# Routing logits and ranks moved to another PSUM bank and to other steps of the attention turns

## The reference, cut to what matters

```
x = LN(x + attention0(x))      16 heads of 64, causal, 2 null keys per head, l2-normed q and k, ALiBi
x = LN(x + moe0(x))            router of 8 experts, argmax: each row goes to one expert
x = LN(x + attention1(x))      squared-distance attention over the 4 batches
x = LN(x + moe1(x))            16 experts, top 2, and a shared one
```

## Time and profile before

| | us |
|---|---|
| median of 3 runs | 1722.08 |
| lowest, highest | 1718.21, 1733.55 |
| the profiled execution, its own time | 1720.87 |
| its span, first to last instruction | 1719.2 |
| TensorE busy | 1524.1 (89%) |
| VectorE busy | 1022.5 (59%) |
| ScalarE busy | 767.5 (45%) |
| GpSimd busy | 533.0 (31%) |
| mean granted TensorE clock | 0.929 |

### The profile page before, as it was taken

One profiled execution on the slowest core, in us unless ns is written; L12 is line 12 of the kernel. 1 busy time (PEld: TensorE's weight loads), 2 busy tenths in 40 slices (PEclk: granted clock), 3 DMA queues, 4 the chain that ended last, 5 costly groups with the idle time before them and its releaser, 6 DMA issues. The chain is left out here.

```text
span 1719.2 us, 26245 instructions
## 1 busy us (share of the span) xinstructions
PE 1524.1 (89%) x8079; PEld 704.2 (41%) x8079; DVE 1022.5 (59%) x2227; ACT 767.5 (45%) x1425; POOL 533.0 (31%) x589
## 2 busy tenths in 40 slices
PE   4899999999999999999999999998399439999997
PEld 2343344444444344443443434344277324444432
DVE  6455555655566664666555576565433267788774
ACT  3445454454544554544354454544044224444432
POOL 2043341533534444244353424432200321111000
PEclk8899899999999999998899999989599759999999
DMA  3503030320202202022020200000411100000000
GB/s 113 180 1 94 7 100 1 113 71 1 71 6 73 90 1 71 1 71 73 5 77 1 72 13 1 10 2 6 164 52 55 34 12 7 13 13 13 7 6 13
DMA packets 106708, 73.73 MB, mean 43 GB/s; under 512 B 5249, under 2 KB 100761, under 8 KB 106318
## 3 DMA queue, kind: packets, MB, share of 16 engines
q1 hardware_dynamic: 104526, 67.85, 13.1%
q0 software_dynamic: 2048, 4.20, 0.8%
HBM read 24.32 MB, written 47.71 MB: 42 GB/s over the span
## 5 line engine op out<-in xcount | busy, mean ns | idle before, releaser
L868 ACT ACTIVATE P<-S,keyb 128x258 f32<-128x258 f32 (+10 forms) x572 | 305.6, 592 | 401.5 <-PE S L635 294.3
L635 PE MATMUL S<-QT,KT 64*128 64x512 f32 (+5 forms) x1792 | 370.1, 494 | 7.1 <-DVE KT L1053 5.6
L1328 POOL TENSOR_SCALAR_AFFINE_SELECT P<-P 128x256 f32<-128x256 f32 (+1 forms) x256 | 162.0, 633 | 494.3 <-ACT P L868 493.6
L1095 DVE TENSOR_TENSOR Psum<-Psum,P 128x1796 f32<-128x1796 f32 (+7 forms) x256 | 283.1, 1106 | 43.6 <-POOL P L1328 30.5
L662 PE MATMUL O<-P,V 128*64 128x512 f32 (+5 forms) x1536 | 263.7, 448 | 4.5 <-POOL P L1328 3.9
L635 PEld LDWEIGHTS S<-QT,KT 64*128 64x128 f32 (+1 forms) x1792 | 161.0, 185 | 231.2 <-issue 227.3
L1305 POOL TENSOR_TENSOR rn<-nm,half 128x8 f32<-128x8 f32 (+1 forms) x120 | 220.6, 1842 | 90.7 <-DVE R L1008 47.3
L496 PE MATMUL W<-xT,wts 128*128 128x512 f32 x256 | 142.1, 650 | 10.1 <-DVE QT L1049 6.8
L662 PEld LDWEIGHTS O<-P,V 128*64 128x64 f32 (+1 forms) x1536 | 82.0, 139 | 113.9 <-issue 100.2
L1162 DVE TENSOR_TENSOR part<-W,rden 128x512 f32<-128x512 f32 x128 | 82.5, 686 | 77.1 <-PE W L711 76.1
L868 ACT ACTIVATE Psum<-S,keyb 128x1024 f32<-128x1024 f32 (+5 forms) x84 | 70.9, 911 | 125.9 <-issue 64.2
(11 more groups left out here) (263 smaller groups left out, 2006.7 us busy)
## 6 DMA issues: line engine op xcount, KB each, us to landing
xg<-zero SPq DMA_DIRECT2D x16, 1216.0 KB, 10.3
yg<-zero SPq DMA_DIRECT2D x16, 1216.0 KB, 9.3
wts<-in_w_qkv SPq DMA_DIRECT2D x16, 384.0 KB, 4.1
gu<-in_gu SPq DMA_DIRECT2D x1, 2816.0 KB
xb<-xg SPq DMA_DIRECT2D x40, 64.0 KB, 1.8
yg<-yb SPq DMA_DIRECT2D x40, 64.0 KB, 1.6
X<-in_x SPq DMA_DIRECT2D x4, 512.0 KB, 5.5
wo<-in_w_out SPq DMA_DIRECT2D x16, 128.0 KB, 2.4
```

The source lines that it names most:

```text
L635: last = nc.tensor.matmul(S[hh][0:m, at + c:at + c + w], KT[d, r, p, jt * P:jt * P + m], QT[d, r, p, Q0[jt] + c:Q0[jt] + c + w], start=Tru ...
L868: last = nc.scalar.activation(probs(p, jt)[0:m, hh, lo:hi], S[hh][0:m, at + lo:at + hi], ACT.Exp, bias=keyb[0:m, r, col:col + 1])
L1095: nc.vector.tensor_tensor(x, x, probs(p, jt)[0:m, :, 0:NQ[jt]], ALU.add).then_inc(add_ok, 1)
L1328: nc.gpsimd.affine_select(own, own, [[0, 2], [1, w]], ALU.is_ge, 0.0, base=NNULL if jt == 0 else 0, channel_multiplier=-1).then_inc(cut, 1)
```

## The change

Three lines are changed. XL moves from step 14a, bank 0, to step 10b, bank 1. XK moves from step 15b, bank 0, to step 14b, bank 1. These are the steps and the bank of E0 and E1. The row sums turned in step 11 (`masses_turned`, bank 1) now wait, in a routing turn, until XL is emptied, that is until the pick is done.

```
             AT = {"P00": "0b", "P01": "0b", "P02": "1b", "P03": "2a", "N0": "3b", "T0": "4b", "V3": "4b", "P10": "5a", "P11": "5b",
-                  "P12": "6a", "P13": "6b", "V0": "7a", "XR": "7b", "V1": "8a", "N1": "8b", "T1": "9b", "V2": "9b", "E0": "10b",
-                  "R0": "11a", "S00": "12b", "S01": "12b", "S02": "13b", "S03": "13b", "XL": "14a", "E1": "14b",
-                  "R1": "15a", "XK": "15b", "S10": "16a", "S11": "16b", "S12": "18a", "S13": "18a"}
-            BANK = dict(zip(AT, (0, 1, 1, 0, 0, 0, 1, 1, 0, 1, 0, 1, 0, 0, 1, 0, 1, 1, 0, 0, 1, 0, 1, 0, 1, 0, 0, 1, 0, 0, 1)))
+                  "P12": "6a", "P13": "6b", "V0": "7a", "XR": "7b", "V1": "8a", "N1": "8b", "T1": "9b", "V2": "9b", "E0": "10b", "XL": "10b",
+                  "R0": "11a", "S00": "12b", "S01": "12b", "S02": "13b", "S03": "13b", "E1": "14b", "XK": "14b",
+                  "R1": "15a", "S10": "16a", "S11": "16b", "S12": "18a", "S13": "18a"}
+            BANK = dict(zip(AT, (0, 1, 1, 0, 0, 0, 1, 1, 0, 1, 0, 1, 0, 0, 1, 0, 1, 1, 1, 0, 0, 1, 0, 1, 1, 1, 0, 1, 0, 0, 1)))
...
                     if ahead:
-                        k = PREP_BEFORE[p][1]
-                        pe.wait_ge(prep_ev[1], emptied(t + 1 + p, k if k in jobs(t + 1 + p) else "V2"))
+                        n = t + 1 + p
+                        k = next(j for j in ("XL", "E0", "V2") if j in jobs(n)) if p == 0 else PREP_BEFORE[p][1]
+                        pe.wait_ge(prep_ev[1], emptied(n, k))
```

## The result

| | us |
|---|---|
| changed kernel, median of 20 runs | 1732.41 (1724.32 to 1740.4) |
| kernel before, median of 20 runs | 1724.5 (1717.11 to 1733.55) |
| ratio | 1.0045, 95% interval 1.003 to 1.0059 |
| profiled execution of the changed kernel | 1727.98, span 1726.2, clock 0.926 |

The change makes the kernel slower by 0.45%, some 8 us. The forecast was 1721 with a range to 1730.

A forecast was written before the change was run, and what follows sets the result against it. Bounds: TensorE around step 10, then VectorE's pace before R1 and the ranks, and the granted clock. Gains of 2 x 0.12 + 4 x 0.15 = +0.8 us took the median from 1722.08 to 1721 us, range 1712 to 1730.

The forecast's parts named there:

- R1's and the ranks' waits: TensorE's idle 1.93 us before R1 and 0.55 before the ranks would go; S10 would wait 2.2 to 2.5 us instead.
- S02 to S10: Stretch from step 13's scores to the first spreading matmul of step 16: forecast 7.4 to 7.8 us, against 8.70 in turn 5.
- The sum of fixed terms: All gains and losses over six routing turns: middle +0.8 us gained, low -2.1, high +3.8.
- the one on the clock: TensorE's idle time per turn is 2.48 us before, 2.49 after, so no reason for fewer or more slow stretches.
- +0.15 us per turn: Middle gain for the already slow turns 9, 10, 13 and 14, between -0.51 and +0.82, as slow stretches shift behind S10.
- The cost of a slow stretch: Time a turn loses to lowered clock: 3.8 us for a long stretch after S10, 3.3 for turn 9 as a whole.
- the unlucky clock: Rival: turn 6 gets a slow stretch (+3.8), turn 5 a longer one, four others lose 0.5 each; 1729 us, 5%.
- The pick as the last wait: Rival: in step 10 the pick ends too late and delays R0's copies, bringing new slow stretches; 1751 to 1758 us, 4%.
- the unreleased R1: Rival: R1 still waits for VectorE in order, so 1.93 us stays and 0.99 is spent per turn; 1728 us, 3%.
- waits that vanish without a follower: Rival: the waits go with none at S10, saving 8.9 us in six turns plus 16 of slow stretches; 1697 us, 3%.
- lucky clock: Rival: the single gap falls so that most slow stretches stay away, saving up to 16 us; 1706 us, 5%.
- GpSimd's cuts: Step 14's cut runs slower beside VectorE's adds (0.94 against 0.41 us); possible 3.2 us loss over six turns, counted as none.

The follow-up runs named there:

- e3: Changed kernel plus six unneeded matmuls in the gap ahead of S10 in the six routing turns; 1715.09 us, 0.9941 of the kernel before.
- e4: Kernel before plus six unneeded matmuls ahead of R1 in the six routing turns; 1711.0 us, 0.9935 of the kernel before.
- g1: Changed kernel with R1 held in routing turns until VectorE's add of step 12, giving two gaps again; 1722.59 us, 0.9992 of the kernel before.
- e1: Kernel before with only the logits' bank changed to 1, still at step 14a; 1728.71 us, 1.0023 of the kernel before.
- f4: Changed kernel with unneeded matmuls ahead of S10, six in routing turns and four in nine others; 1695.91 us, 0.9843 of the kernel before.
- e2: Changed kernel with the ranks put back at step 15b, bank 0, so only the logits are moved; 1734.1 us, 1.0066 of the kernel before.
- f2: Changed kernel plus two unneeded matmuls ahead of S10 in routing turns, held until VectorE's add of step 13; 1731.62 us, 1.0044 of the kernel before.

## Why the prediction was wrong

**What held.** The logits cost 0.99 us at step 10, exactly. The pick delayed nothing there. R1's and the ranks' waits went and one of S10 took their place, 2.42 us for the 2.2 to 2.5 named. S02 to S10 takes 7.67 us, within 7.4 to 7.8. At full clock the turns are as long as before to 0.02 us (e3 and e4, turns 5 and 6). The sum of fixed terms, a gain of 0.8 us between -2.1 and +3.8, had the right size; the heights say a loss of 1.7 us, e3 against e4 a gain of 0.5.

**The step that failed** is the one on the clock: "I see no reason for fewer slow stretches, or for more", because TensorE's idle time is 2.48 us before and 2.49 after. I counted the idle time by its sum. At full clock the sum is the same, and in g1 it is the same again, but in one gap ahead of S10 it comes with 17 us more at 1.2 GHz in a mean run, 5.4 us of run time by the slope. g1 gives them back by a wait alone, and filling takes away most of the difference. e1 loses 14 us of clock with hardly any work moved, but its profile doesn't show that its longer gap draws them. Why the same idle time draws more slow time there than ahead of R1 stays open.

**A term of the sum was mis-sized too**: the +0.15 us per turn for turns 9, 10, 13 and 14, "since no row tells how much of the stretch will fall where". In turn 13, with a long stretch in both kernels, it is 74.88 - 75.40 = -0.52, the low end of -0.51 that the prediction gave. All of the stretch came back behind S10, where no such wait covers it. The 1.7 us between the heights fit this; one turn is too little to show that it is all of them.

**The cost of a slow stretch** was right in size (3.3 to 3.8 us for a long one; turn 6 lost 4.0). The price of one was known; how many there would be I took from one execution of each case. Five of six before and six of six after is a difference that one profile can't show, and the mean clock of many runs does.

**The rivals.** The nearest was the unlucky clock, 1729, which I gave 5% as an accident, while it was the ordinary case. Its terms mostly held: +3.8 us for turn 6 (4.0) and +0.5 for a turn that stays slow (turn 13). The pick as the last wait, the unreleased R1 and waits that vanish without a follower were all wrong. Of "lucky clock" the price was about right: e4 is 12 us under before, of up to 16.

**The range** ended at 1730 for a median of 1732.4. Of the 11.4 us between the forecast and the median, 2.4 are that the median of 20 runs of the kernel before is 1724.5 and not the 1722.08 of three. That alone puts the median past the end of the range, so it is chance that it lies just outside and not just inside. The other 9 us are that the medians differ by 7.9, where a gain of 1 was forecast; that goes to the two steps above.

GpSimd's cuts did run slower beside the adds, as the earlier trace rows let expect: the cut at 489.20 us in turn 5 takes 0.94 us, against the 0.41 of the earlier trace rows. With turns as long as before at full clock, that costs nothing.

## What to carry to other kernels

When a wait is taken away, write down where the idle time goes, beside which other gap it comes to lie and what waits behind it, even if the path doesn't change: the same idle time can cost more granted clock in another place, and a slow stretch costs less where a wait follows that it can use up. Judge such a change by the mean clock of many runs, or by a pair in which both kernels have their gaps filled; one profile of each can't tell. And before moving work to shorten a wait of 2 us in an otherwise busy TensorE, try what unneeded matmuls in the gap give: here 1.6%, more than any of the moves.

## What was not expected of the hardware

- The run time follows the time at 1.2 GHz with 0.328 us per us, over 14 kernels from 170 to 275 us of it; what is left scatters by 1.2 us. The price depends on what follows: a long stretch costs 3.3 us in turn 13 before the change (74.88 us against 71.56 at full clock in e4), where a wait is used up, and 3.9 with it (75.40 against 71.54 in e3).
- The gap's size acts unevenly: 2.42 and 1.98 us draw the same slow time (263 and 268 us), 1.54 draws 233, and 1.11 draws 219, with no slow stretch in the six turns of e3's profile and a short one in f4's turn 13.
- The same idle time of 2.4 to 2.5 us per routing turn at full clock comes with 247 us at 1.2 GHz where the larger part stands ahead of R1 and the rest 1.2 or 1.6 us of matmuls later (before, g1), and with 263 where all of it stands ahead of S10. Whether it is the parting or the place that counts isn't shown: e1 and e2 part it with their larger gap late, and have 261 and 275. f2, 1.31 and 0.40 us with 0.7 us of matmuls between them, has 265.
- Filling one gap per turn in 15 of the 16 attention turns takes the mean run from 1731.4 to 1697.3 us.
